# One layer moved from the layers' stream into the search's, and one weave table per engine

## The reference, cut to what matters

```python
x = L0_attn_x
xn = _layernorm(x, axis=-1)
s = _L0_attn_ref(xn, ...)          # gated scan over time, 16 heads of 8
g = _silu(_L0_ffn_ref(xn, ...))    # three cycles of a small coupling net
x = x + s * g
...                                # L1: time mix; windowed attention, twice
...                                # L2: selective scan (16 states); 4 experts, 2 kept
xn = _layernorm(x, axis=-1)
s = _L3_attn_ref(xn, ...)
g = _silu(_L3_ffn_ref(xn, ...))    # the coupling net again
x = x + s * g
```

```python
q = _layernorm(q, q_gamma, q_beta); k = _layernorm(k, k_gamma, k_beta)
scores = jnp.einsum('bhnd,bhmd->bhnm', q, k) / jnp.sqrt(jnp.float32(D))
aw = jax.nn.softmax(scores, axis=-1)
kth = jax.lax.top_k(aw, topk)[0][..., -1:]       # topk = 25 of 512
aws = aw * (aw >= kth); aws = aws / (aws.sum(-1, keepdims=True) + 1e-08)
o_s = jnp.einsum('bhnm,bhmd->bhnd', aws, v)
...                                              # o_l: linear attention with softmaxed q, k
o = a * o_s + (1.0 - a) * o_l
```

## Time and profile before

| | us |
|---|---|
| median of 3 runs | 5811.5 (5808.37 to 5865.23) |
| the profiled execution, its own time | 5860.5 |
| its span, first to last instruction | 5858.7 |
| mean granted TensorE clock, share of full | 0.767 |
| busy: PE / DVE / ACT / POOL | 4234.7 / 3994.7 / 3039.3 / 2527.5 |

### The profile page before, as it was taken

How to read it: one execution, slowest core, us unless ns; L and a number is a source line. 1 busy time by engine, 2 the same in 40 slices (tenths; PEclk the granted TensorE clock), 3 DMA queues, 4 the chain that set the end, 5 groups by cost and what they waited for, 6 DMA issues and landing times. The chain is left out here.

```text
span 5858.7 us, 58221 instructions
## 1 busy us (share of the span) xinstructions
PE 4234.7 (72%) x16676; PEld 1933.8 (33%) x16676; DVE 3994.7 (68%) x7874; ACT 3039.3 (52%) x5809; POOL 2527.5 (43%) x2356
## 2 busy tenths in 40 slices
PE   5776777767777677766777677776777767777676
PEld 1331234323342234422343223432244322332233
DVE  3325567776677766776667857678566786677798
ACT  3434455555555555545554555555555554565543
POOL 1103244454445344453443534436344363444466
PEclk8885788778886888858778678876787768887655
DMA  1000000000000000000000000000000000000000
GB/s 72 1 22 0 4 1 22 1 1 5 1 22 0 3 3 1 22 0 3 3 1 22 0 3 3 22 1 0 5 1 22 1 0 5 1 22 1 2 1 3
DMA packets 7995, 44.07 MB, mean 8 GB/s; under 512 B 848, under 2 KB 848, under 8 KB 7248
## 3 DMA queue, kind: packets, MB, share of 16 engines
q1 hardware_dynamic: 7632, 39.89, 1.8%
HBM read 37.52 MB, written 2.36 MB: 7 GB/s over the span
## 5 line engine op out<-in xcount | busy, mean ns | idle before, releaser
L2105 POOL TENSOR_SCALAR top<-top,m 128x512 f32<-128x512 f32 x512 | 808.1, 1578 | 1255.3 <-DVE m L2042 1171.5
L2042 DVE MAX8 m<-top 128x8 f32<-128x512 f32 x2048 | 1292.9, 679 | 8.3 <-ACT top L1972 7.6
L2046 DVE MATCH_REPLACE8 top<-m,top 128x512 f32<-128x512 f32 x1536 | 1026.0, 675 | 0.2
L296 PE MATMUL bank<-arena,weights 128*128 128x512 f32 (+7 forms) x1200 | 689.5, 688 | 286.8 <-ACT arena L510 56.6
L296 PE MATMUL bank<-arena,consts 128*128 128x512 f32 (+1 forms) x966 | 713.6, 835 | 72.9 <-POOL arena L1643 23.6
L2111 POOL TENSOR_TENSOR top<-top 128x512 f32<-128x512 f32 x512 | 661.6, 1292 | 24.5 <-ACT top L1980 6.5
L1910 PE MATMUL bank<-consts,top 128*128 128x128 f32 x2048 | 420.7, 342 | 247.2 <-POOL top L2111 192.5
L296 PE MATMUL bank<-arena 128*64 128x128 f32 (+4 forms) x3328 | 502.9, 370 | 119.9 <-ACT arena L1084 61.7
L1987 ACT ACTIVATE top<-bank 128x512 f32<-128x512 f32 x512 | 304.9, 596 | 473.8 <-PE bank L1910 473.3
L317 ACT ACT_TABLE_LOAD x358 | 459.3, 1283 | 110.3 <-PE bank L296 102.0
L1910 PEld LDWEIGHTS bank<-consts,top 128*128 128x128 f32 x2048 | 302.5, 175 | 569.6 <-POOL top L2111 341.3
(11 more groups left out here) (261 smaller groups left out, 6377.0 us busy)
## 6 DMA issues: line engine op xcount, KB each, us to landing
arena<-experts_dram SPq DMA_DIRECT2D x32, 768.0 KB, 6.6
weights<-weights_dram SPq DMA_DIRECT2D x1, 6982.0 KB, 19.6
hold<-x_dram SPq DMA_DIRECT2D x9, 256.0 KB, 2.7
out_dram<-x_out SPq DMA_DIRECT2D x9, 256.0 KB, 3.5
consts<-consts_dram SPq DMA_DIRECT2D x1, 1759.5 KB, 23.3
rot<-consts_dram SPq DMA_DIRECT2D x1, 1024.0 KB, 25.3
```

The costliest lines, as they stand in the source:

```text
L296: return nc.tensor.matmul(o, lhsT, rhs, start=start, stop=stop)
L2042: nc.vector.max(m8[:, slot(p, e), k], src).then_inc(SB["top"], 1)
L2046: nc.vector.match_replace(wk_[e], m8[:, slot(p, e), k], sc[slot(p, e)] if k == 0 else wk_[e], -3e38).then_inc(SB["rest"], 1)
L2105: nc.gpsimd.tensor_scalar(pp[e], sc[slot(p, e)], m8[:, slot(p, e), TOPK // 8, 0:1], None, ALU.is_ge).then_inc(SB["kept"], 1)
```

## The change

- Layer 3 is taken out of `a_*` and put at the head of `b_*`: a pass now runs opening, layers 0, 1 and 2 of one item beside layer 3 and the search of the item before. Its 21 steps make the search's stream 264 steps long. The first block has no layer 3, the last one has it in front of the search.
- The opening goes to the head of `l0_*`. The small block for the first item is gone; x0 of item 0 is loaded in the set-up, with the others in the pass before, and SP waits for it there.
- Layer 3 works in `top` and in the banks X, Y and P of the search instead of in `arena` and A, with `xn_b` (the tile `oo`) as its normalised input. It writes `vt`, `ol`, `kf` and `th_b` directly, and ACT makes the four masked `qm` from PE's bank. So the copies of `kf`, `q_t`, `vt`, `ol` and `th` go; POOL keeps the copy of x.
- Since `top` and the banks are shared, the search's first maximum, mask and value product wait for layer 3's gate, its first fetch for `ol`.
- `weave` takes a table per engine: the n-th character (base 36) is the number of search steps behind the n-th yield of the layers' stream (200 yields).
- `table` takes further sets that would also do (`table(GELU, TANH, SILU)` in front of a tanh), and is called ahead of the wait nearly everywhere.

```diff
-ROOM = {"hop": 1.8, "l0": 1.0, "pj": 0.8, "at0": 0.8, "at1": 0.8, "at2": 0.7, "wo": 1.5, "ffn": 1.3,
-        "moe": 1.5, "state": 0.1, "states": 0.1, "busy": 0.3}
-def weave(a, b):
-    room = 0.0
-    for kind in a or ():
-        room += ROOM[kind]
-        while b is not None and room >= 1.0:
-            room -= 1.0
+SEARCH = {"PE": ("0020014070211016030010100001a401000500224111213032a0003007101041001121000228104210023120310147012010"
...
+def weave(a, b, places):
+    for n, _ in enumerate(a or ()):
+        for _ in range(int(places[n], 36) if b is not None and n < len(places) else 0):
             next(b, None)
     for _ in b or ():
         pass
...
-        def table(name):
-            if now[0] != name:
+        def table(name, *also):
+            if now[0] != name and now[0] not in also:
                 nc.scalar.preload_act_table_set(name)
                 now[0] = name
...
                 for k in range(3):
+                    table(GELU)
                     a.wait_ge(*S("cn1", k + 1))
-                    table(GELU)
                     act(self.h1, b, ACT.Gelu, bias=W(lay + "_cn_b1")).then_inc(S["cn1_gelu"], 1)
...
+                    table(GELU, TANH, SILU)
                     a.wait_ge(*S("cn4", k + 1))
                     if k:
                         a.wait_ge(*S("cycle_c", k))
-                    table(GELU)
                     act(self.th, b, ACT.Tanh, bias=couple[:, n, 0:1], scale=0.5).then_inc(S["tanh"], 1)
...
+            yield from L.op.pe(pe)
             cp = L.cp.pe(pe)
+            pe.wait_ge(*S("op_kn", 1))
+            pe.wait_ge(*S("op_qn", 1))
             mm(A[1], W("l0_Wv"), xn0).then_inc(S["v"], 1)
...
             if not first:
-                v.wait_ge(*SB("taken", 4))
-                v.wait_ge(*SB("mask", 5))
+                v.wait_ge(*S3("taken", 1))
+                v.wait_ge(*S3("xn_xc", 1))
             tt(x[:], x0, L.m, ALU.add).then_inc(S["x_new"], 1)
...
             def __init__(L):
-                L.carve = Carve(0, EDGE)
+                L.carve = Carve(0, 14 * T, top)
...
-                act(kf_n, A[1], ACT.Identity, scale=by_channel[:, 1:2], bias=by_channel[:, 3:4]).then_inc(S["kf"], 1)
+                act(kf[:], F[1], ACT.Identity, scale=by_channel[:, 1:2], bias=by_channel[:, 3:4]).then_inc(S["kf"], 1)
                 a.wait_ge(*S("qk_turn", 2))
-                act(q_t, A[0], ACT.Copy).then_inc(S["qt"], 1)
+                for r in range(4):
+                    act(qm[:, r], F[0], ACT.Identity, scale=keep[:, 0, r:r + 1], bias=keep[:, 2, r:r + 1]).then_inc(S["mask"], 1)
...
+            yield from l3_pe(pe)
             yield
             score(0)
...
             def fetch(p, e):
+                if p == 0:
+                    a.wait_ge(*S3("ol", 1))
                 a.wait_ge(*SB("score", p + 1))
...
+                    if p == 0:
+                        v.wait_ge(*S3("gate", 1))
                     v.wait_ge(*SB("sc", 2 * p + e + 1))
...
-            nc.gpsimd.tensor_copy(vt[:], vt_n).then_inc(SB["taken"], 1)
-            nc.gpsimd.tensor_copy(ol[:], ol_n).then_inc(SB["taken"], 1)
-            nc.gpsimd.tensor_copy(th_b[:], th_n).then_inc(SB["taken"], 1)
-            nc.gpsimd.tensor_copy(x_b[:], x[:]).then_inc(SB["taken"], 1)
+            yield from l3_pool(g)
...
             yield from l2_pe(pe)
-            yield from l3_pe(pe)
...
                         sp.dma_start(x0, x_in[b + 1]).then_inc(SD["x0"], 16)
+                        sp.wait_ge(SD.sem["x0"], 16)
                         sp.wait_ge(*S1("attn", DEPTH))
```

More of the change, by code:

```diff
@@ L335, in build @@
             marks = Marks(nc, c0, "setup")
-            S = marks.layer(DMA="loaded 3", PE="by_channel 1", ACT="exp_a 1,alpha 1",
+            S = marks.layer(DMA="loaded 4", PE="by_channel 1", ACT="exp_a 1,alpha 1",
                             DVE="head_sum 2,head_mean 1,by_channel_sb 1")
@@ L754, in l0_act @@
             S, L = S0, Layer0
+            yield from L.op.act(a)
             cp = L.cp.act(a)
@@ L812, in l0_pool @@
             S, L = S0, Layer0
+            yield from idle("hop hop hop hop hop hop hop hop")
             cp = L.cp.pool(g)
@@ L1028, in time_mix @@
                 yield
+                table(TANH, GELU, SILU)
                 a.wait_ge(*S("r", i + 1))
-                table(TANH)
                 act(L.sr, A[3], ACT.Tanh, scale=0.5).then_inc(S["sr"], 1)
@@ L1455, in l2_act @@
                 if n < NE * FCH:
+                    table(SILU)
                     a.wait_ge(*S("w1", n + 1))
@@ L1784, in l3_act @@
                 yield "hop"
-            op = L.op.act(a)
-            for n, _ in enumerate(op):
-                if n == 3:
-                    if not first:
-                        a.wait_ge(*SB("taken", 4))
-                    L.cp.act_silu(a, th_n)
-                yield "hop"
+            L.cp.act_silu(a, th_b[:])
         def l3_dve(v):
@@ L1873, in l3_dve @@
                 yield "hop"
-            for _ in L.op.dve(v):
-                yield "hop"
         def l3_pool(g):
+            nc.gpsimd.tensor_copy(x_b[:], x[:]).then_inc(S3["taken"], 1)
             yield from idle("hop hop hop")
@@ L1880, in l3_pool @@
                 yield "hop"
-            yield from idle("hop hop hop hop hop hop hop hop")
         def place(p):
@@ L1987, in take @@
                 act(pt_[e], Y, ACT.Copy).then_inc(SB["pt"], 1)
-            act(kf[:], kf_n, ACT.Copy).then_inc(SB["mask"], 1)
-            for r in range(4):
-                act(qm[:, r], q_t, ACT.Identity, scale=keep[:, 0, r:r + 1], bias=keep[:, 2, r:r + 1]).then_inc(SB["mask"], 1)
+            yield from l3_act(a)
             yield
@@ L2153, in a_act @@
             yield from l2_act(a)
-            yield from l3_act(a, first)
         def a_dve(v, first):
@@ L2159, in a_dve, with a_pool @@
             yield from l2_dve(v)
-            yield from l3_dve(v)
-        def a_pool(g, first):
-            if not first:
-                g.wait_ge(*SB("mask", 5))
+        def a_pool(g):
             yield from l0_pool(g)
@@ L2167, in a_pool @@
             yield from l2_pool(g)
-            yield from l3_pool(g)
         def run(b, item, search):
```

218 lines of the change are left out of this document (101 added, 117 removed).

## The result

The changed kernel takes 5558.4 us (median of 4, 5552.5 to 5565.5), the kernel before 5835.5 in the same comparison (4 runs, 5808.4 to 5865.2): ratio 0.9525, 95% interval 0.9462 to 0.9587. The forecast was 5.9% faster (5470 against 5811.5), the result is 4.7%. The profiled execution took 5554.5 us, where the forecast's sum for it was 5515.

The account below looks back on a forecast made before the run. No engine was full; a chain hopping between engines, delayed by search steps, bound the pass. Passes of 658 instead of 703.7 us (-320) and ends (-25) took 5860.5 to 5515, times 0.9916 gives 5470 us; range 5380 to 5650.

Parts of the forecast that it names:

- Price per step times steps: Whole pass: each stage's time alone plus its search steps at the old weave's price per step, 682.7 us in sum.
- First stretch: Pass start to the end of layer 0: opening, part of layer 3, then layer 0 with 34 search steps, 147.8 us.
- Before the scan: Layer 2 up to its scan: 85.2 us alone plus 34 search steps at 0.75 us, 110.7 us.
- Scan 99.1: Layer 2's scan: 79.6 us alone plus 30 steps at 0.65, 99.1 us; DVE's busy time a floor of 96.6.
- Seven of the saved loads: ACT's table loads: of 15 saved a pass, seven vanish with layer 3, already held in the solo durations.
- Loads ahead of their waits: ACT's remaining 32 loads a pass, issued before their waits: up to 9.3 us a pass saved, half taken, 4.6.
- Tables -10, loads saved -10.3: Per-engine tables shorten a pass by 10 us; eight loads saved in layers 1 and 2 give 10.3 us.
- The ends: First block 86.0 us shorter, last block 62 longer, x0 1 at most, loads -2: net -25 us.
- POOL against DVE: More DVE work beside POOL work: taken as nothing; by the shared-port rule up to 10 us a pass longer.
- A: Start of a pass: search waits for layer 3's gate and holds up layer 0; pass 680, total 5622 us; chance 0.18.
- B: Layers 1 and 2: denser weaving costs half as much a step; pass 619, total 5199 us; chance 0.20.
- C: Layer 1 and before layer 2's scan: bursts cost 0.81 us a step; pass 721, total 5907, 1.6% slower; chance 0.12.

Follow-up runs that it names:

- the third run: The changed kernel with the old weave, its numbers of room for all engines scaled by 1.29: 5676.5 us, ratio 0.9726 to the kernel before.

## Why the prediction was right or wrong

The direction and most of the size were right, though several terms were wrong and offset each other. In the profiled execution the sum was 39 us short: seven passes of 662.9 instead of 658 are 34 of them, the ends the other 5. Step by step:

- *Price per step times steps, the pass with old prices 682.7.* This is the move without the tables and the loads, and the run of the move alone has 686.5. That the two agree is partly luck: the kernel divides its steps otherwise (20 ahead of layer 0's loop, 38 in layer 0, 133 in layer 1, 67 before the scan, 4 in it). With its measured 81.6 up to layer 0 the prices give 81.6 + 94.7 + 310.5 + 135.5 + 82.2 + 5.6 = 710. Layer 1 took 311 there, as priced; layer 0 took 76 instead of 95 and the stretch before the scan 127 instead of 135.5. The prices of those two stages were too high for this order, so that the move is worth more than I computed.
- *First stretch 147.8.* Measured 138.1. Layer 0 starts at 47.9, not 56.4, and then takes 90.2 against 91.4. The failed term is "all four engines have 14 steps in front of layer 0": that holds for its loop, but on PE only 7 of them stand ahead of its first product, and on DVE 12 ahead of its first instruction. The opening and layer 3 overlap more than my 22 + 31.3.
- *Layer 1, 319.5.* Measured 323.3. The price of 0.475 rose to 0.50 with half as many steps again: (323.3 - 247.3) / 152.
- *Before the scan, 110.7.* Measured 101.3, a price of 0.47 instead of 0.75. My 0.75 held reloads: before, ACT had 13 loads there against 5 alone, now 9. Eight loads are at most 10.3 of the 38.3 us that the 51 steps had cost, so they don't explain all of the fall; the rest is open.
- *Scan 99.1, with DVE as a floor of 96.6.* Measured 94.7, below the floor. The guest steps brought 82.7 - 61.3 = 21.4 us of DVE, not 35.1: the last two of the 34 rounds have no maxima any more (16 MAX8 and 12 MATCH_REPLACE8 are 18.2 of the 21.4 us), so 1.17 us a step was the wrong mean for just these steps, and the floor was no floor.
- *Seven of the saved loads go with layer 3.* Wrong. With the old weave the changed kernel has 49 loads a pass, two more than before. The move saves none; all 17 are the tables' doing: the order puts fewer switches between the search's exponentials and the layers' GELU and SILU.
- *Loads ahead of their waits 4.6 us.* 4.9 under the old weave (686.5 to 681.6), but 11.9 under the tables (674.8 to 662.9). In the kernel before 31 us in all, 4.4 a pass, but there the trace shows missing long passes and not shorter ones. Half of the loads' time was right in one order only. A load had no one price in these runs: 0.15 us each for the 243 of the tables, 0.47 for those of the old weave, 1.07 for the doubled ones.
- *Tables -10, loads saved -10.3.* Together 20.3, measured 681.6 - 662.9 = 18.7. That the sum came out is luck: 8 loads were counted where 17 were saved, and by the two kernels without reloads the place of the steps gives nothing once no reload is left. So the gain hangs on the loads. That it is their number alone isn't shown: 37 and 39 loads a pass went with 5963 and 5763 us, 49 with 5677. The reason I gave, POOL a round too early, found no support: POOL two steps later made the kernel 11% slower.
- *The ends, -25.* First block -86.0 as forecast; last block +65.5 instead of 62; together -20.5. That the first block came out at 86.0 is partly chance. The same first block, with no search in it, took 529.2 to 536.1 us in the traces of six kernels with loads ahead of their waits, and 540.8 and 539.2 in the two with loads behind. The changed kernel's own is the longest of the six (layer 1 alone took 250.0 in it, 246.0 in the third run). So the loads' place is worth 3 to 12 us there, where I had put 2.
- *TensorE and the drain behind a load.* The mechanism from the Trainium skill (ScalarE: Activation LUTs, What ACT_TABLE_LOAD costs) would have made a load cost 2.66 us. The doubled loads cost 269 us for 252, 1.07 each, but they stand back to back and so don't test what lies between a load and an operation; that is the earlier trace rows, with 20 ns. No run here shows the drain.
- *POOL against DVE.* DVE's busy time of a pass is 499.6 now and was 498.4, so nothing, as taken. The rule of the page (SBUF — State Buffer, SBUF: two separate sides, of the Trainium skill) shows at single instructions only. The last L1615 of before (1737 ns in the middle of eight) starts at 5439.29, 0.07 us behind a POOL product that takes 1.27. In the changed kernel the same line is L1621; in the last pass POOL starts nothing in the 3 us behind its last product of layer 2, and the line is short in all eight blocks:

```profile
L1621 DVE SCALAR_TENSOR_TENSOR arena<-arena,weights x8: 752/753/753, 523.8 to 5166.1; 128x512 f32<-128x512 f32 x8
```
- *Rivals.* A didn't occur: layer 0 took its 90. B would have needed layer 1 under 290. C's place and price do exist, in another kernel: DVE's table for all engines has 0.69 us a step in layer 1 and ends 2% slower than before, with a pass of 721.8 where C had 721. The turning point of 0.74 was near it.
- *From 5515 to 5470.* I scaled the sum by 0.9916, as the profiled execution of before was 0.8% above its median. Wrong for the kernel after: two passes of 720 us had made that execution long, the changed kernel has no such passes, and its profiled execution (5554.5) is at its median (5558.4). These 45 us are over half of the 88 that the total was off.

What stays open: why even filling of the stages (39 loads, 5763) is worse than the old weave (49 loads, 5677), and how much of the tables' gain is the number of loads and how much is where they fall. It would need a kernel with the tables' order and 49 loads, which was not run.

## What to carry to other kernels

Before a table of orders is judged by its waits, count the reloads it leads to: here 17 of 49 loads a pass went with the order, and with no reloads left the tables' gain was gone. The count alone is no measure of an order, as 37 and 39 loads went with slower kernels. Issue a load ahead of the wait of what it serves: in the changed kernel that was worth 50 and 86 us; in the kernel before it went with the absence of the two long passes, and took no more than 3 us off any other. A stream that is woven into a chain can be priced per step from stages with and without it, a price that held in layer 1 (0.475 and 0.50) and in the changed kernel's layer 0, was too high in layer 2, and rose to 0.69 under another order of the same steps. Forecast from passes, not from an execution scaled to a median, where passes come in two lengths. A long wait of an engine with spare time was not a reason to delay that engine, as all others then waited for it.

## What the runs showed of the hardware

A pass of the kernel before takes 696 us or 720 with the same instructions. Most of the difference is in layer 1, here in the last pass but one and in the last (busy us by stretch of the kernel before, columns as in the earlier trace rows; the second row stands there):

```profile
4226.60:4541.40 314.80, 243.47 (x1168) 126.85 (x1168) 206.17 (x449) 167.13 (x378) 137.15 (x140) 0.78 0.03 12
```

DVE, ACT and POOL are busy for the same time in both; PE's 1168 products take 243 us instead of 221, at a mean granted clock of 0.78 instead of 0.87 of full speed. What tips a pass to one side no run here shows. The changed kernel's seven passes lie within 8.2 us of each other. The kernel before takes 5808 to 5878 us over all comparisons, and its medians in the four are 5830 to 5857, so a change below 1% is hard to see beside it.
